# Two selected feed-forward stages of an eight-stage transformer kernel: all sequences normalised and transposed ahead, and the first product of the next sequence issued before the second product of this one

## The reference, cut to what matters

```
def ffn(hidden_states, Wp1, bp1, Wp2, bp2, W1, b1, W2, b2, Wo, bo):   # hidden_states: (8, 256, 128), already normalised
    last = hidden_states[:, -1, :]
    logits = gelu(last @ Wp1 + bp1) @ Wp2 + bp2                       # (8, 8): one choice for each sequence
    sel = argmax(softmax(logits), axis=-1)
    w1, w2 = W1[sel], W2[sel]                                         # one expert of eight for each sequence
    h = gelu(hidden_states @ w1 + b1[sel])                            # (8, 256, 256)
    reasoned = h @ w2 + b2[sel]                                       # (8, 256, 128)
    return hidden_states + 0.3 * (reasoned @ Wo + bo)
x = x + layernorm(ffn(layernorm(x), ...))
```

## Time and profile before

| | |
|---|---|
| Median of 3 runs | 1131.25 us (1130.49 to 1139.63) |
| The profiled execution | 1135.26 us, of which its span in the profile is 1133.4 us |
| Busy: PE, DVE, ACT, POOL | 82%, 64%, 51%, 41% of the span |
| Mean granted TensorE clock | 0.913 of full speed |
| Stage of layer 1, first to last instruction | 542.8 to 586.6 us |
| Stage of layer 2, first to last instruction | 876.3 to 921.4 us |

### The profile page before, as it was taken

One profiled execution on the slowest core, in us unless ns is written; L12 is line 12 of the kernel. 1 busy time (PEld: TensorE's weight loads), 2 busy tenths in 40 slices (PEclk: granted clock), 3 DMA queues, 4 the chain that ended last, 5 costly groups with the idle time before them and its releaser, 6 DMA issues. The chain is left out here.

```text
span 1133.4 us, 23807 instructions
## 1 busy us (share of the span) xinstructions
PE 930.7 (82%) x7973; PEld 726.8 (64%) x7988; DVE 725.7 (64%) x2000; ACT 572.4 (51%) x1192; POOL 464.1 (41%) x528
## 2 busy tenths in 40 slices
PE   6899895699993789889779999999997767539990
PEld 5566664689983655655667666767666655428990
DVE  4678645676665866774557667666644668856664
ACT  2667662346652576765354555454442445325662
POOL 2366663563444212221361333343343442575442
PEclk9899996799996998999799999999999977658995
DMA  9211110121212112111400011111021620012214
GB/s 294 69 53 52 52 54 1 41 72 47 58 29 75 39 59 59 59 58 42 138 27 1 2 40 40 40 39 32 10 57 21 239 85 1 21 54 66 60 46 111
DMA packets 80767, 66.42 MB, mean 59 GB/s; under 512 B 6706, under 2 KB 73457, under 8 KB 80267
## 3 DMA queue, kind: packets, MB, share of 16 engines
q1 hardware_dynamic: 76139, 56.45, 17.5%
q0 software_dynamic: 4512, 8.47, 2.2%
HBM read 38.76 MB, written 26.58 MB: 58 GB/s over the span
## 5 line engine op out<-in xcount | busy, mean ns | idle before, releaser
L454 DVE TENSOR_REDUCE a_rowmax<-a_banks 128x4 f32<-128x1024 f32 (+1 forms) x112 | 136.7, 1222 | 58.9 <-PE a_banks L721 27.3
L2378 POOL TENSOR_TENSOR a_both<-a_probs 128x512 f32<-128x512 f32 x64 | 86.3, 1348 | 159.8 <-ACT a_probs L2603 159.8
L576 ACT ACTIVATE a_probs<-a_banks 128x1024 f32<-128x1024 f32 x112 | 115.0, 1026 | 58.2 <-PE a_banks L707 47.2
L1243 POOL DMA_INDIRECT acc<-m_result,m_yb x77 | 75.5, 980 | 96.4 <-DVE m_result L1560 52.6
L2603 ACT ACTIVATE a_probs<-a_banks 128x1024 f32<-128x1024 f32 x64 | 65.6, 1025 | 88.5 <-PE a_banks L2662 88.5
L2509 DVE TENSOR_REDUCE a_rowmax<-a_banks 128x4 f32<-128x1024 f32 x64 | 78.0, 1220 | 15.0 <-PE a_banks L2639 14.9
L1236 POOL DMA_INDIRECT rows<-m_yrow,m_idx x64 | 64.7, 1010 | 45.6 <-issue 21.1
L1673 ACT ACTIVATE m_gate<-m_banks 128x352 f32<-128x352 f32 (+1 forms) x93 | 42.9, 461 | 72.7 <-PE m_banks L1862 72.7
L2676 PE MATMUL a_banks<-a_probs,a_V 128*64 128x256 f32 x512 | 69.4, 392 | 0.6 <-ACT a_craw L2592 0.6
L1888 PE MATMUL m_banks<-e_down,m_hT_hi 128*128 (+2 forms) x231 | 65.3, 351 | 0.6 <-DVE m_hT_lo L1543 0.6
L749 PE MATMUL a_banks<-a_probs,a_V 128*32 128x256 f32 x720 | 59.2, 401 | 6.9 <-ACT a_raw L564 6.4
(11 more groups left out here) (382 smaller groups left out, 2746.0 us busy)
## 6 DMA issues: line engine op xcount, KB each, us to landing
rows<-fill SPq DMA_DIRECT2D x16, 520.0 KB, 4.3
a_factor<-recip_rows SPq DMA_DIRECT2D x28, 256.0 KB, 4.6
rows<-fill SPq DMA_DIRECT2D x15, 455.0 KB, 4.0
m_yb<-rows SPq DMA_DIRECT2D x77, 65.0 KB, 1.8
f_expert<-in_experts SPq DMA_DIRECT2D x16, 257.5 KB, 3.0
m_parts<-acc SPq DMA_DIRECT2D x16, 256.0 KB, 5.0
e_gu_lo<-in_gu SPq DMA_DIRECT2D x1, 2736.0 KB
e_last_row<-in_last_rows SPq DMA_DIRECT2D x1, 2736.0 KB
```

The lines of the kernel that those rows point to most:

```text
L454: nc.vector.reduce_max(o, src, AX).then_inc(rowmax_ready, 1)
L576: nc.scalar.activation(probs[h][:, k, :, :], ps[:, 4:6, :], ACT.Exp, scale=SCALE).then_inc(exp_done, 1)
L1243: nc.gpsimd.indirect_dma_start(acc.rearrange("k n d -> (k n) d"), bass.IndirectOffsetOnAxis(yb[b % YB][:, P:P + 1].bitcast(U32), 0), resul ...
L2378: nc.gpsimd.tensor_tensor(both[u % 4][:, :, :], p[:, :, 0, :], p[:, :, 1, :], ALU.add).then_inc(both_ready, 1)
```

## The change

All of it is in `selected_ffn`, so it acts in both stages.

- `y` and `yT` get 8 buffers each, one for each sequence; `yb` is gone, and POOL adds the bias in place in `y`, after PE has transposed it (`with_bias` waits for `yT_ps`). The waits for a free buffer go.
- The input statistics and the power are done for two sequences at a time: four `bn_stats`, four `bn_aggr`, one epsilon addition and one power of 128 x 4.
- DVE does all `in_moments` and all `normed` before its loop. In the loop remain `f`, the output statistics and `t`.
- `t = (f - mean) * rstd` moves from ACT (two instructions of 128x128) to DVE (two tensor_scalar), and `shift` goes. POOL adds `t` into `x` one pass sooner.
- ACT's loop becomes: gelu of `s + 1`, `yT` of `s + 5`, `rT` of `s`.
- PE: `turned(1)`, `busy(5)`, `turned(2)`, `turned(3)`, `busy(5)` take the place of `busy(12)`. Then come the first product of 0 and `turned(4)`, and the loop body becomes: first product of `s + 1`, output product of `s - 1`, `turned(s + 5)`, second product of `s`. `busy(26)` at the end stays.

```diff
-        y = [st.sb(f"y{k}", [P, T, P]) for k in range(3)]
-        yb = [st.sb(f"yb{k}", [P, T, P]) for k in range(2)]
-        yT = [st.sb(f"yT{k}", [P, SEQ]) for k in range(2)]
+        y = [st.sb(f"y{k}", [P, T, P]) for k in range(SEQS)]
+        yT = [st.sb(f"yT{k}", [P, SEQ]) for k in range(SEQS)]
...
@@ POOL
             def with_bias(i):
-                pool.wait_ge(y_ready, i + 1)
-                if i >= 2:
-                    pool.wait_ge(f_ready, i - 1)
-                nc.gpsimd.tensor_tensor(yb[i % 2][:, :, :], y[i % 3][:, :, :],
+                pool.wait_ge(yT_ps, i + 1)
+                nc.gpsimd.tensor_tensor(y[i][:, :, :], y[i][:, :, :],
...
             in_power(0)
-            in_power(1)
...
-            in_power(2)
+            in_power(1)
             pool.wait_ge(bo_ready, 1)
             with_bias(0)
             with_bias(1)
-            for s in range(SEQS + 4):
+            in_power(2)
+            with_bias(2)
+            in_power(3)
+            for s in range(SEQS + 3):
                 if s + 3 in ahead:
-                    in_power(s + 3)
-                if s + 2 in ahead:
-                    with_bias(s + 2)
+                    with_bias(s + 3)
...(output power of s - 1)
-                if s - 3 in ahead:
-                    i = s - 3
+                if s - 2 in ahead:
+                    i = s - 2
                     pool.wait_ge(t_ready, i + 1)
...(x = x + t)
@@ DVE
             in_moments(0)
-            in_moments(1)
...(statistics of the last tokens, normed(0), y_last, normed(1))
-            in_moments(2)
+            in_moments(1)
...(logits, maximum, index)
-            for s in range(SEQS + 3):
-                if s + 2 in ahead:
-                    normed(s + 2)
-                if s + 3 in ahead:
-                    in_moments(s + 3)
+            normed(2)
+            normed(3)
+            for k in (2, 3):
+                in_moments(k)
+                normed(2 * k)
+                normed(2 * k + 1)
+            for s in range(1, SEQS + 2):
...(f and output statistics of s - 1)
                 if s - 2 in ahead:
                     i = s - 2
                     dve.wait_ge(out_rstd, i + 1)
-                    nc.vector.scalar_tensor_tensor(shift[:, i, :], mv["out"][:, i, :, 0], -1.0, rstd["out"][:, i, :],
-                                                   ALU.mult, ALU.mult).then_inc(shift_ready, 1)
+                    if i >= 2:
+                        dve.wait_ge(x_done, i - 1)
+                    for j in range(T):
+                        last = nc.vector.tensor_scalar(t[i % 2][:, j, :], f[i % 3][:, j, :], mv["out"][:, i, j, 0:1],
+                                                       rstd["out"][:, i, j:j + 1], ALU.subtract, ALU.mult)
+                    last.then_inc(t_ready, 1)
@@ ACT
+            for i in range(1, 4):
+                to_sbuf(i)
+            hidden(0)
+            to_sbuf(4)
+            for s in range(SEQS):
+                if s + 1 in ahead:
+                    hidden(s + 1)
+                if s + 5 in ahead:
+                    to_sbuf(s + 5)
...(rT of s)
@@ PE
-            busy(12)
+            turned(1)
+            busy(5)
+            turned(2)
+            turned(3)
+            busy(5)
...
+            first(0)
+            turned(4)
             for s in range(SEQS + 1):
+                if s + 1 in ahead:
+                    first(s + 1)
+                if s - 1 in ahead:
+                    output(s - 1)
+                if s + 5 in ahead:
+                    turned(s + 5)
                 if s in ahead:
...
+                    second(s)
             busy(26)
```

More of the change, by code:

```diff
@@ L2084, in _, with moments @@
             nc.vector.tensor_scalar(bo[:, :], at["bo"], 0.3, None, ALU.mult).then_inc(bo_ready, 1)
-            def moments(k, i, src, done):
-                for j in range(T):
-                    last = nc.vector.bn_stats(stats[k][:, i, j, :], src(j))
+            def moments(k, of, src, done):
+                for i in of:
+                    for j in range(T):
+                        last = nc.vector.bn_stats(stats[k][:, i, j, :], src(i, j))
                 steps.after(last)
@@ L2091, in moments, with in_moments @@
                 own_wait(dve, st.dve_waited)
[L2092 to L2093 removed]
+                for i in of:
+                    for j in range(T):
+                        last = nc.vector.bn_aggr(mv[k][:, i, j, :], stats[k][:, i, j, :])
                 steps.after(last)
                 steps.wait(dve)
[L2096 to L2099 removed]
+                some = slice(of[0], of[-1] + 1)
+                nc.vector.tensor_scalar(var[k][:, some, :], mv[k][:, some, :, 1], EPS, None, ALU.add).then_inc(done, 1)
+            def in_moments(k):
+                moments("in", [2 * k, 2 * k + 1], lambda i, j: x[:, i * T + j, :], in_var)
             def normed(i):
[L2102 to L2105, removed]
+                dve.wait_ge(in_rstd, i // 2 + 1)
                 for j in range(T):
[L2107 removed]
+                    last = nc.vector.tensor_scalar(y[i][:, j, :], x[:, i * T + j, :], mv["in"][:, i, j, 0:1],
                                                    rstd["in"][:, i, j:j + 1], ALU.subtract, ALU.mult)
@@ L2162, in to_sbuf, with hidden @@
                 act.wait_ge(yT_ps, i + 1)
+                nc.scalar.activation(yT[i][:, :], ps[:, i % 2, 0:SEQ], ACT.Copy).then_inc(yT_ready, 1)
+            def hidden(i):
+                act.wait_ge(expert_loaded[i], 16)
+                act.wait_ge(h_ps, i + 1)
                 if i >= 2:
-                    act.wait_ge(h_ps, i - 1)
-                nc.scalar.activation(yT[i % 2][:, :], ps[:, i % 2, 0:SEQ], ACT.Copy).then_inc(yT_ready, 1)
+                    act.wait_ge(r_ps, i - 1)
+                for c in range(2):
+                    last = nc.scalar.activation(hT[i % 2][:, c, :], ps[:, 2 + i % 2, c * SEQ:(c + 1) * SEQ], ACT.Gelu,
+                                                bias=ex[i]["b1"][:, c:c + 1])
+                last.then_inc(h_ready, 1)
             act.wait_ge(y_lastT_ps, 1)
@@ L2171, in _ @@
             nc.scalar.activation(nav[:, :], ps[:, 7, 0:SEQS], ACT.Gelu, bias=at["nav_b"]).then_inc(nav_ready, 1)
[L2172 to L2181, removed]
-                if s + 1 in ahead:
[L2183 to L2198, removed]
+            for i in range(1, 4):
[3 more added lines that the diff above has]
+            for s in range(SEQS):
+                if s + 1 in ahead:
+                    hidden(s + 1)
+                if s + 5 in ahead:
+                    to_sbuf(s + 5)
+                act.wait_ge(r_ps, s + 1)
+                if s >= 2:
+                    act.wait_ge(out_ps, s - 1)
+                nc.scalar.activation(rT[s % 2][:, :], ps[:, 4 + s % 2, 0:SEQ], ACT.Identity, bias=ex[s]["b2"]).then_inc(
+                    r_ready, 1)
         @block.tensor
@@ L2226, in _ @@
             mm(ps[0:SEQS, 6, 0:NE], nav[:, :], at["choose_w"], start=True, stop=True).then_inc(logit_ps, 1)
-            busy(12)
-            for s in range(SEQS + 1):
-                if s in ahead:
[L2230 to L2256, removed]
@@ new lines, in _, with first, output @@
+            turned(1)
[3 more added lines that the diff above has]
+            busy(5)
+            def first(i):
+                pe.wait_ge(expert_loaded[i], 16)
+                pe.wait_ge(yT_ready, i + 1)
+                for c in range(2):
+                    last = mm(ps[:, 2 + i % 2, c * SEQ:(c + 1) * SEQ], ex[i]["w1"][:, c * P:(c + 1) * P], yT[i][:, :],
+                              start=True, stop=True)
+                last.then_inc(h_ps, 1)
+            def output(i):
+                pe.wait_ge(r_ready, i + 1)
+                if i >= 2:
+                    pe.wait_ge(f_ready, i - 1)
+                for j in range(T):
+                    last = mm(ps[:, 6 + i % 2, j * P:(j + 1) * P], rT[i % 2][:, j * P:(j + 1) * P], at["wo"], start=True,
+                              stop=True)
+                last.then_inc(out_ps, 1)
@@ new lines, in second @@
+            def second(i):
+                pe.wait_ge(h_ready, i + 1)
+                for c in range(2):
+                    last = mm(ps[:, 4 + i % 2, 0:SEQ], ex[i]["w2"][:, c * P:(c + 1) * P], hT[i % 2][:, c, :], start=c == 0,
+                              stop=c == 1)
+                last.then_inc(r_ps, 1)
+            first(0)
+            turned(4)
+            for s in range(SEQS + 1):
+                if s + 1 in ahead:
[4 more added lines that the diff above has]
+                    turned(s + 5)
+                if s in ahead:
+                    second(s)
```

21 lines of the change are left out of this document (10 added, 11 removed).

## The result

The changed kernel is faster by 0.87%: ratio to the kernel before 0.9913, 95% interval 0.9886 to 0.994, from 13 runs of each. The ratio leaves out the slowest execution of the changed kernel, 1139.86 us, which lies over 1.5% above its fastest; with it the ratio of the means is 0.9925. On this base of 1131 to 1135 us that is 9.9 us (6.8 to 13); the forecast was 8.7, and no change beyond 1% was given the largest chance. The plain medians are 1128.97 us and 1135.09 us, 6.1 us apart; the 1131.25 shown ahead of the prediction was the median of its first three runs. A second set on another chip gave 0.991 (0.9882 to 0.9937).

A forecast was written before the change was run, and what follows sets the result against it. PE's wait for the gelu inside each pass was taken as the bound. Gains of 4.5 us in layer 1 and 4.2 in layer 2, the later beginning included, sum to 8.7: 1131.25 - 8.7 = 1122.5 us, range 1116 to 1130.

The forecast's parts named there:

- no change beyond 1%: Whole kernel: time within about 1% (11.3 us) of the kernel before, given chance 0.60.
- The beginning: Start of the stage: norms now stand before the loop on DVE, making the second product of 1 1.95 us later.
- The three collisions: Before the loop: tensor_scalar pairs held up by POOL's bias additions, costing 0.87 + 0.35 + 0.87 = 2.1 us a stage.
- The hold that `shift` had shown: DVE stands still beside a POOL addition: `shift`, 0.16 us alone, took 0.68 in the kernel before.
- the rule cited from the Trainium skill: GpSimd contends with DVE instructions in a two-port mode or with two SBUF inputs; `f` and bn_stats are not exposed.
- The loop: Gelu stall goes; the 2.98 us pass shrinks to 2.40 with transposes and 2.18 without, bounded by PE.
- its margin of 0.04: In the loop: output product may start 1.70 us after the second product's start, while PE's two products take 1.74.
- rival 2: Loop pass stays at 2.98 us because `rT` comes late; gain only 0.8 a stage, 1129.6 us; chance 0.08.
- The 1.6 us at the end of the stage: Layer 2's end: 8.15 us instead of 6.52 at a fallen clock; possible 1.6 gain, counted as nothing.
- 1: Beginning of the stage: POOL collisions cost less, 2.1 us a stage shorter; with the clock's gain 1116.7 us; chance 0.13.
- 3: Beginning: PE clock falls or stays low; 2.5 us lost, 2.2 more each further pass; taken as 1127 us; chance 0.18.
- 4: Loop: DVE becomes the bound, `t` held by POOL, pass 3.4 us, stage ends 2.9 later; 1137 us; chance 0.09.

## Why the prediction was right

By its steps, in layer 1, counted from the first product of 0:

| | predicted | measured |
|---|---|---|
| `y` of 4 lets `turned(4)` go | 2.15 | 2.21 |
| Second product of 1 | 7.05 | 7.07 |
| Pass with, without transposes | 2.40, 2.18 | 2.39, 2.17 |
| Output product of 7 (the stretch) | 22.0 | 21.89 |
| From there to the end of the filler | 6.52 | 6.52 |

These distances are the evidence that the mechanism was right; the total alone, with an interval from 6.8 to 13 us, would not be.

**The beginning.** Its price was 1.95 us against the kernel before, and is 1.97. The three collisions were put at 2.1; the rows give 0.82 + 0.41 + 0.83 = 2.06 over 1.11. The hold that `shift` had shown applied to tensor_scalar as laid out, and `f` and bn_stats were free: `f` took 0.42 at 561.57 beside an addition, as in the earlier trace rows, and four bn_stats 0.86 with the moved additions. That agrees with the rule cited from the Trainium skill ("GPSIMD Engine Reference", section 1, Specifications).

**The loop.** Both pass lengths came out, and `rT` with its margin of 0.04 stayed hidden while first products stood between; rival 2 did not happen.

**The cause was right as far as it went, and one bound was missing from it.** "So PE has 2.40 us of work in a pass of 2.98. The rest is the loop first product, gelu, second product" held: with the norms ahead in the old order the passes stay at 2.97. "Later passes grow longer, since ACT also makes `t`" is borne out too. In the kernel before:

```profile
571.94 1.03 PE L2235 MATMUL f_banks<-f_yT,f_expert 128*128 128x256 f32 x4
...
572.87 0.88 ACT L2196 ACTIVATE f_t<-f_f,f_shift,f_out_rstd 128x128 f32<-128x128 f32 x2 [0.25 <-DVE f_shift L2153]
...
573.65 0.82 ACT L2179 ACTIVATE f_hT<-f_banks,f_expert 128x256 f32<-128x256 f32 x2
```

The gelus of 4 to 7 start 1.34, 1.35, 1.71 and 2.03 after their first products, instead of 1.12, each right behind `t` in ACT's stream. That is 0.2, 0.2, 0.6 and 0.9 late, and the last four passes are as much over 2.97 (3.19, 3.18, 3.55, 3.86). For the last two `t` was late itself, as it waited for `shift`. No run takes `t` off ACT and leaves all else as it was, so this rests on these rows. What the prediction never added up is a pass of DVE and POOL in the kernel before: up to 4.20, longer than any pass of PE. It did not matter for the sum, because the change takes away both bounds at once and the schedule was worked out with both gone. It matters for whoever takes the gelu wait for the whole cause: the order alone made the stretch 1.1 to 1.3 longer.

**Layer 2 and the clock.** The 1.6 us at the end of the stage were taken at nothing. Between the two profiles they came in full, 8.15 to 6.52; with them the forecast would have been 10.3. Whether the change did it stays open: the kernel before has one profile, and every variant with 26 filler products ended layer 2 in 6.5, the new order alone too, whose stretch is longer still.

The two stages gave 5.1 and 6.0 in the profile, against 4.5 and 4.2, 2.4 more. Of this, 1.6 is the clock. Another 0.3 is a slip in the prediction: it moved the steps by 333.5, the distance of the two stages' starts, but the first products of 0 lie 333.2 apart (886.73 less 553.55), so its 4.2 should have been 4.5. The stretches gave about 0.2 more than forecast. The rest is the time from the stage's start to the first product of 0: 10.77 to 10.34 in layer 1, and 10.42 to 10.66, the other way, in layer 2. In the second profile of the changed kernel it was 10.57 and 10.65, so part of the gain in layer 1 is scatter. What sets it was not tested.

**Rivals.** 1: the collisions did not cost less; what it promised, 2.1 a stage, had to be made by moving the additions, and 1.9 of it came. 3: PEclk in the loop was 1.00 throughout. In layer 2 the first ten filler instructions took 2.34 us at the lower clock, where layer 1's took 1.28, and it cost nothing: the transposes behind them start 1.49 after `normed(2)` (879.20 less 877.71), in layer 1, where PE waited for `y`, 1.47 (550.10 less 548.63):

```profile
876.81 2.34 PE L2215 MATMUL f_banks<-ident 128*128 128x128 f32 x10
...
879.98 1.28 PE L2215 MATMUL f_banks<-ident 128*128 128x128 f32 x10
```

4: `t` takes 0.60 in each pass, and was held once a stage, at the very end (1.00 at 577.52), where PE's filler covers it.

**The base.** The forecast time, 1122.5, was subtracted from the median of three runs. The changed kernel's median over 13 is 1129.0, just under the range's upper end of 1130; the ratio, which puts it 9.9 us under the kernel before, is what can be compared with the 8.7.

## What to carry to other kernels

When a reordering removes the wait that the profile shows, look for what each engine's own pass adds up to with that wait gone: here PE's pass of 2.97 us with the gelu wait hid a ring of DVE and POOL that already took 4.18, and either edit by itself left the stretch where it was or longer. A late result costs only what stands behind it in a queue, so put late work behind ready work first, then make it early. Place GpSimd additions beside DVE work that reads PSUM or computes statistics, not directly behind the result that frees a tensor_scalar.

## What the runs showed of the hardware

The stretch repeats to 0.3 us between two profiles of the changed kernel on two chips (21.89 and 21.66, 21.93 and 21.93), and to 0.1 where two kernels differ in the filler at the end alone. Whole executions of one kernel vary by about 20 us and go with the mean granted clock of TensorE: on one chip the kernel before took 1127.62 us at 0.923 and 1142.92 at 0.907. Between chips its median was 1135, 1138, 1158 and 1161. Where it was 1158, the changed kernel had its two stages unchanged and the rest of the program longer, with a lower clock in some stretches: from 200 to 300 us it was granted 0.90 in its first profile and 0.80 in the second, and PE was busy for 88.5 and 80.9 us.

For a change of some us in one stage, the stage's own distances in the profile tell more than the total.
